# Second attention of a two-layer block: one of four score banks of four steps in eighteen is exponentiated on VectorE, and the products run four steps behind

## The reference, cut to what matters

```python
# four sequences of 1024 tokens, 128 channels, 16 heads of 8
xn = layernorm(x)
s = L0_attn(xn)                  # layer norm, qkv, softmax(q k / sqrt(8)) v, out projection, residual
g = silu(L0_ffn(xn))             # relu^2 MLP, five spiking steps, mean spike count
x = x + s * g
xn = layernorm(x)
# second layer
q, k, v = heads(xn @ W + bias)   # [4, 16, 1024, 8]
attn = q @ k.T / sqrt(8) - slope[h] * (1023 - key)
attn = where(causal, attn, -max)
p = softmax(attn)                # the exponentials that the change splits over two engines
s = (p @ v) @ Wo + bo
g = silu(L1_ffn(xn))             # three cycles of a coupling network
return x + s * g
```

## Time and profile before

| what | value |
|---|---|
| median of 3 runs | 917.85 us |
| profiled execution, its own time | 918.43 us |
| its span, first to last instruction | 916.5 us |
| mean granted TensorE clock | 0.973 |
| ACT busy, share of the span | 830.1 us, 91% |
| PE busy | 796.1 us, 87% |
| DVE busy | 406.5 us, 44% |
| POOL busy | 208.5 us, 23% |

### The profile page before, as it was taken

The page is one execution under the profiler, slowest core; times in us unless marked ns, Lnnn a source line. Parts: engine busy times, 40 slices in busy tenths (PEclk is TensorE's granted clock), DMA queues, the critical chain, the costliest instruction groups (busy, mean ns, idle before and its releaser), DMA issues. The chain is left out here.

```text
span 916.5 us, 23114 instructions
## 1 busy us (share of the span) xinstructions
PE 796.1 (87%) x9838; PEld 320.2 (35%) x9838; DVE 406.5 (44%) x878; ACT 830.1 (91%) x919; POOL 208.5 (23%) x261
## 2 busy tenths in 40 slices
PE   4849999899999999998999988856888888878977
PEld 2412434234343443433334433212333333333423
DVE  7821255443757446484545777880121121121122
ACT  7759999999999999999999956646999999999996
POOL 2201110130202212021211202002234334324333
PEclk9969999999999999999999999985999999999999
DMA  6882020200301202103000043010112022022000
GB/s 181 283 278 37 2 75 3 75 2 2 98 25 28 95 1 75 48 2 120 2 1 25 24 121 136 0 46 1 29 47 86 10 78 86 1 86 86 2 13 25
DMA packets 32048, 53.51 MB, mean 58 GB/s; under 512 B 5576, under 2 KB 16456, under 8 KB 31944
## 3 DMA queue, kind: packets, MB, share of 16 engines
q1 hardware_dynamic: 31944, 52.02, 18.0%
HBM read 31.29 MB, written 20.71 MB: 57 GB/s over the span
## 5 line engine op out<-in xcount | busy, mean ns | idle before, releaser
L973 ACT ACTIVATE a_probs<-a_sc 128x1024 f32<-128x1024 f32 x512 | 474.1, 1032 | 9.5 <-PE a_sc L1172 9.2
L1843 ACT ACTIVATE a_probs<-a_sc 128x1024 f32<-128x1024 f32 x288 | 270.0, 1041 | 23.8 <-PE a_sc L1995 17.2
L1187 PE MATMUL a_o<-a_probs,vt 128*18 128x256 f32 (+1 forms) x3072 | 271.6, 457 | 0.0
L2030 PE MATMUL a_o<-a_probs,vt 128*18 128x256 f32 (+3 forms) x1856 | 154.6, 442 | 0.9
L1172 PE MATMUL a_sc<-q_st,k_st 32*128 32x512 f32 x1024 | 131.0, 500 | 23.3 <-ACT a_probs L973 17.9
L1989 PE MATMUL a_sc<-q_st,k_st 32*128 32x512 f32 (+3 forms) x768 | 79.3, 428 | 56.8 <-ACT a_probs L1843 45.5
L1869 POOL TENSOR_SCALAR_AFFINE_SELECT a_probs<-a_probs 128x512 f32<-128x512 f32 x128 | 80.6, 648 | 194.7 <-ACT a_probs L1843 194.7
L1187 PEld LDWEIGHTS a_o<-a_probs,vt 128*18 128x18 f32 x3072 | 65.2, 97 | 143.2 <-issue 102.9
L1172 PEld LDWEIGHTS a_sc<-q_st,k_st 32*128 32x128 f32 x1024 | 50.4, 183 | 137.7 <-ACT a_probs L973 128.3
L1000 POOL TENSOR_TENSOR early<-early 128x512 f32<-128x512 f32 x32 | 38.3, 1198 | 179.2 <-DVE early L1110 179.2
L1902 DVE STREAM_TRANSPOSE a_turn<-a_o 128x512 f32<-128x512 f32 x15 | 10.8, 717 | 152.5 <-PE a_o L2030 152.5
(11 more groups left out here) (242 smaller groups left out, 754.9 us busy)
## 6 DMA issues: line engine op xcount, KB each, us to landing
q_st<-q_hl SPq DMA_DIRECT2D x48, 256.0 KB
k_st<-k_hl SPq DMA_DIRECT2D x48, 256.0 KB
q_hl<-parts SPq DMA_DIRECT2D x12, 512.0 KB, 4.3
k_hl<-parts SPq DMA_DIRECT2D x12, 512.0 KB, 4.7
q_hl<-early SPq DMA_DIRECT2D x4, 512.0 KB, 4.8
k_hl<-early SPq DMA_DIRECT2D x4, 512.0 KB, 5.2
out_dram<-x SPq DMA_DIRECT2D x7, 256.0 KB, 3.9
x<-in_L_attn_x_dram SPq DMA_DIRECT2D x3, 512.0 KB, 5.9
```

What stands on the lines that cost most here:

```text
L973: nc.scalar.activation(probs[t % RING][:, 2 * pair:2 * pair + 2, :], scores[unit % SLOTS][:, :, :], ACT.Exp).then_inc(expd, 1)
L1187: ins = nc.tensor.matmul(o_ps[32 * h:32 * h + 2 * W9, c0:c1], vt[b % 2][:, kt, gp, h, W9 * gs:W9 * gs + 2 * W9], probs[t % RING][:, h, c0: ...
L1843: nc.scalar.activation(probs[t % RING][:, 2 * pair:2 * pair + 2, :], scores[unit % SLOTS][:, :, :], ACT.Exp).then_inc(expd, 1)
L2030: ins = nc.tensor.matmul(o_ps[32 * h:32 * h + 2 * W9, q0:q0 + w], vt[b % 2][:, kt, gp, h, W9 * gs:W9 * gs + 2 * W9], probs[t % RING][:, h, ...
```

## The change

Four edits go together.

1. In the second attention the steps 5, 7, 14 and 16 of each group of 18 (`TAKES`) have their fourth head's bank exponentiated by DVE (`raise_head`): seven instructions that build the exponential from the bit pattern of a scaled score and a polynomial in its fraction. ACT's second ACTIVATE of such a step covers one head, 512 columns, in place of two. `score(t)` on PE also waits for the first of the seven instructions of step t-2, and `product(t)` for the last of its own step's.
2. LAG1 goes from 2 to 4 and the ring from 4 to 6. The two new buffers are the tiles `early`, and two scratch rows lie in `ext`.
3. In both attentions a multiply packs a lifted bank's used columns of both `gp` into one tile `gathered`, and only the second `gp` is transposed back. `on` has two tiles in place of four, the output weights are packed without zero rows (8 loads in place of 16, no memsets), and `mix` has half of the matmuls, in one piece: at pairs 4 and 15 of the second attention, 4 and 27 of the first.
4. At the end of the second attention four matmuls before the last two banks go away. POOL's early part of the last half (step 24) also waits for an earlier update.

```diff
+def gather(nc, ends, turned, recip, gathered, gp):
+    used = turned.rearrange("p (n r) -> p n r", r=32)[:, :, 0:2 * W9].rearrange("p n (s r) -> p n s r", r=W9)
+    ends.after(nc.vector.reciprocal(recip, used[:, :, :, D]))
+    blocks = turned.shape[1] // 32
+    ends.mark(nc.vector.tensor_tensor(gathered[:, :, gp, :, :], used[:, :, :, 0:D],
+                                      recip.rearrange("p n (s o) -> p n s o", o=1).broadcast_to([P, blocks, 2, D]), ALU.mult))
...
-            fill("mix", b - 1, 1, 3, 4)
+            fill("mix", b - 1, 1, 4)
...
-                    ends.after(nc.vector.reciprocal(recip[:, :, :], used[:, :, :, D]))
-                    ends.after(nc.vector.tensor_tensor(
-                        used, used, recip[:, :, :].rearrange("p n (s o) -> p n s o", o=1).broadcast_to([P, HALF // 32, 2, W9]), ALU.mult))
-                    nc.vector.transpose(on[e % ENDS][:, :], t[:, :]).then_inc(on_rdy, 1)
+                    gather(nc, ends, t[:, :], recip[:, :, :], s["gathered"][hf][:, :, :, :, :], gp)
+                    if gp == 1:
+                        ends.wait()
+                        nc.vector.transpose(on[hf][:, :], s["gathered"][hf][:, :, :, :, :].rearrange("p n g s d -> p (n g s d)")).then_inc(on_rdy, 1)
...
-                        pe.wait_ge(on_rdy, ENDS * b + 2 + hf + 1)
-                        for t in (2 * piece, 2 * piece + 1):
-                            for gp in range(2):
-                                ins = by_columns(nc, side_tiles[:, t, :], on[2 * gp + hf][:, t * P:(t + 1) * P],
-                                                 s["wo_x"][:, gp, :], start=gp == 0, stop=gp == 1)
+                        pe.wait_ge(on_rdy, 2 * b + hf + 1)
+                        for t in range(HT):
+                            ins = by_columns(nc, side_tiles[:, t, :], on[hf][:, t * P:(t + 1) * P], s["wo_x"][:, :])
...
                 for t in range(HT):
-                    for gp in range(2):
-                        ins = nc.tensor.matmul(pb[:, 1, t * C:(t + 1) * C], on[2 * gp + 1][:, t * P:(t + 1) * P],
-                                               s["wo_x"][:, gp, :], start=gp == 0, stop=gp == 1)
+                    ins = nc.tensor.matmul(pb[:, 1, t * C:(t + 1) * C], on[1][:, t * P:(t + 1) * P], s["wo_x"][:, :],
+                                           start=True, stop=True)
...
-LAG1 = 2
+LAG1 = 4
+RING1 = 6
 CORNER = 96
 STEEP = 1
+GROUP_STEPS = 18
+TAKES = (5, 7, 14, 16)
+TAKEN_HEAD = G - 1
+FRACTION, EXPONENT, ONE = 0x007FFFFF, 0x7F800000, 0x3F800000
+BITS_PER_E = float(np.float32(2.0 ** 23 / np.log(2.0)))
+BITS_OF_ONE = float(np.float32((127.0 - 6.2072499967381) * 2.0 ** 23))
+LEADING = 2.0 ** (BITS_OF_ONE / 2.0 ** 23 - 127.0)
+QUARTIC = [float(np.float32(c / LEADING)) for c in (-0.0021252070, 0.16661338, 0.31201603, 0.50996422)]
+POWER_OPS = 7
...
-            fill("mix", b - 1, 1, 3, 4)
+            fill("mix", b - 1, 1, 4)
...
-            fill("mix", b, 0, 14, 15)
...
-    LAST = S // 2 + 2
+    LAST = (S + LAG1) // 2 + 1
...
-        probs = [sb(f"probs{n}", [P, G, HALF]) for n in range(RING)]
+        late = [t[:, :, :, :].bitcast(F32).rearrange("p z n t -> p (z n) t") for t in s["early"]]
+        probs = [sb(f"probs{n}", [P, G, HALF]) for n in range(RING)] + late
+        bits, fraction = (s["ext"][0][:, HALF * n:HALF * n + HALF] for n in range(2))
...
+                    if t >= RING1:
+                        act.wait_ge(pv_done, t - RING1 + 1)
                     for pair in range(2):
                         unit = 2 * t + pair
                         act.wait_ge(scored, unit + 1)
-                        nc.scalar.activation(probs[t % RING][:, 2 * pair:2 * pair + 2, :],
-                                             scores[unit % SLOTS][:, :, :], ACT.Exp).then_inc(expd, 1)
+                        heads = 1 if by_vector(t) and pair == TAKEN_HEAD // 2 else 2
+                        nc.scalar.activation(probs[t % RING1][:, 2 * pair:2 * pair + heads, :],
+                                             scores[unit % SLOTS][:, 0:heads, :], ACT.Exp).then_inc(expd, 1)
...
-                    ends.after(nc.vector.reciprocal(recip[:, :, :], used[:, :, :, D]))
-                    ends.after(nc.vector.tensor_tensor(
-                        used, used, recip[:, :, :].rearrange("p n (s o) -> p n s o", o=1).broadcast_to([P, HALF // 32, 2, W9]), ALU.mult))
-                    nc.vector.transpose(on[e % ENDS][:, :], t[:, :]).then_inc(on_rdy, 1)
+                    gather(nc, ends, t[:, :], recip[:, :, :], s["gathered"][hf][:, :, :, :, :], gp)
+                    if gp == 1:
+                        ends.wait()
+                        nc.vector.transpose(on[hf][:, :], s["gathered"][hf][:, :, :, :, :].rearrange("p n g s d -> p (n g s d)")).then_inc(on_rdy, 1)
...
+                power = Chain(dve, powered)
+                def raise_head(t):
+                    unit = 2 * t + TAKEN_HEAD // 2
+                    out = probs[t % RING1][:, TAKEN_HEAD, :]
+                    if power.n:
+                        power.wait()
+                    dve.wait_ge(scored, unit + 1)
+                    power.after(nc.vector.tensor_scalar(bits.bitcast(U32), scores[unit % SLOTS][:, TAKEN_HEAD % 2, :],
+                                                        BITS_PER_E, BITS_OF_ONE, ALU.mult, ALU.add))
+                    power.mark(nc.vector.tensor_scalar(fraction.bitcast(U32), bits.bitcast(U32), FRACTION, ONE, ALU.bitwise_and, ALU.bitwise_or))
+                    power.after(nc.vector.tensor_scalar(bits.bitcast(U32), bits.bitcast(U32), EXPONENT, None, ALU.bitwise_and))
+                    if t >= RING1:
+                        dve.wait_ge(pv_done, t - RING1 + 1)
+                    power.after(nc.vector.scalar_tensor_tensor(out, fraction, QUARTIC[0], fraction, ALU.add, ALU.mult))
+                    power.after(nc.vector.scalar_tensor_tensor(out, out, QUARTIC[1], fraction, ALU.add, ALU.mult))
+                    power.after(nc.vector.scalar_tensor_tensor(out, out, QUARTIC[2], fraction, ALU.add, ALU.mult))
+                    power.mark(nc.vector.scalar_tensor_tensor(out, out, QUARTIC[3], bits, ALU.add, ALU.mult))
...
                 e = 0
@@ -1950,6 +1995,8 @@
                     ending = e < B * ENDS - 1 and 2 * pair - LAG1 > PER1 * (e // ENDS) + closing[e % ENDS]
                     if ending:
                         lift(e)
+                    if by_vector(2 * pair) and 2 * pair < S:
+                        raise_head(2 * pair)
                     for n, kind, at, hf, piece, pieces in pieces_at(pair):
                         if piece == pieces - 1:
                             evacuate(n, kind, at, hf)
@@ -1959,6 +2006,8 @@
                     for hf in range(2):
                         if b < B and r == GATE_AT[hf]:
                             gate(b, hf)
+                    if by_vector(2 * pair + 1) and 2 * pair < S:
+                        raise_head(2 * pair + 1)
...
-                    for unit in (2 * t, 2 * t + 1):
-                        if unit >= SLOTS:
-                            pe.wait_ge(expd, unit - SLOTS + 1)
+                    for unit in (2 * t - SLOTS, 2 * t + 1 - SLOTS):
+                        if unit >= 0:
+                            pe.wait_ge(expd, unit + 1)
+                            if by_vector(unit // 2) and unit % 2 == TAKEN_HEAD // 2:
+                                pe.wait_ge(powered, POWER_OPS * takes_before(unit // 2) + 1)
...
@@ -2021,6 +2072,8 @@
                             pe.wait_ge(masked, masked_count(t))
                         else:
                             pe.wait_ge(expd, 2 * t + 2)
+                        if by_vector(t):
+                            pe.wait_ge(powered, POWER_OPS * (takes_before(t) + 1))
                         if opens and t > 0:
...
-                        pe.wait_ge(on_rdy, ENDS * b + 2 + hf + 1)
-                        for t in (2 * piece, 2 * piece + 1):
-                            for gp in range(2):
-                                ins = by_columns(nc, side_tiles[:, t, :], on[2 * gp + hf][:, t * P:(t + 1) * P],
-                                                 s["wo_x1"][:, gp, :], start=gp == 0, stop=gp == 1)
+                        pe.wait_ge(on_rdy, 2 * b + hf + 1)
+                        for t in range(HT):
+                            ins = by_columns(nc, side_tiles[:, t, :], on[hf][:, t * P:(t + 1) * P], s["wo_x1"][:, :])
...
-                for t in range(HT):
-                    nc.tensor.matmul(tail_banks[t], on[1][:, t * P:(t + 1) * P], s["wo_x1"][:, 0, :], start=True, stop=False)
...
```

More of the change, by code:

```diff
@@ L846, in side_fills @@
         if b < B:
-            fill("mix", b, 0, 26, 27)
+            fill("mix", b, 0, 27)
         if 0 < b < B:
@@ L1742, in second_fills @@
             fill("z", b, 1, 7)
-            fill("mix", b, 0, 14, 15)
+            fill("mix", b, 0, 15)
     return fills
@@ L1804, in tail_tiles, with takes_before, by_vector @@
```

(12 more changed lines are left out.)

45 lines of the change are left out of this document (18 added, 27 removed).

## The result

| | before | after |
|---|---|---|
| median of 5 runs, same chip | 918.64 us (917.49 to 921.28) | 950.82 us (946.39 to 951.44) |
| profiled execution, span | 916.5 us | 944.1 us |
| mean granted TensorE clock | 0.973 | 0.956 |
| ACT busy, DVE busy | 830.1, 406.5 us | 818.9, 552.0 us |

The ratio is 1.034 with a 95% interval of 1.032 to 1.036: slower by 32 us, where 919.3 us were forecast, and outside the range of 907 to 929. The profiled execution of after is its shortest run, at 946.39 us. In the block, ACT's exponentials run from 622.5 us to about 930.5 us, where they ended at 907.9 before: 23 us more. Behind ACT's last one it takes another 13.6 us to the end of the span, where it took 8.6.

What follows compares the result with a forecast made beforehand. ACT was taken to set the pace: 918.43 - 13.1 (half units) - 4.3 (old stalls) + 17.0 (displaced work) + 3.0 (end) - 1.2 (middle block) = 919.8 us profiled, 919.3 us as median; 8-in-10 range 907 to 929 us.

Steps and rivals of the forecast that it cites:

- ACT's gain: Second attention: 32 units lose one bank, 0.41 us each, saving 13.1 us, with PE keeping up.
- the half unit is not worth 0.41 us: Rival on ACT's half units: saving 0.2 us less per unit leaves 6.7 us missing, partly hidden; 924 us, chance 0.04.
- Steps 14, 16, 32, 34: Second attention: second chain's first instruction, delayed by POOL's update, comes late for PE's scores; ACT loses 2.6 us.
- Chains held by POOL: Rival at the eight lift waits: masks hold chains 0.5 us each; 928 us, 936 with slow bit operations; chance 0.28.
- Steps 23, 25, 5 and 7: Second attention: lifts behind two chains delay PE's products; ACT loses 5.7 us (23, 25) and 8.7 us (5, 7).
- The end: End of second attention: later products and a last chain lengthened by POOL's update cost 3.0 us, bounds 1.9 and 3.7.
- the lag: At the end, products run two steps further behind: six after the last scores, not four, 2 x 0.87 us.
- POOL's part at step 24: Last half's early part: its added wait has only later masks behind it and costs nothing.
- at the start: Fewer PE products while the clock is 0.50: could save or cost 2 us, taken as nothing.
- DVE's chain: The seven DVE instructions of a take last 4.5 us, bounds 4.3 and 5.0.
- Old stalls: Second attention: ACT's losses at first query-half-1 diagonals, 1.24 us x 3 + 0.6 us, go: 4.3 us saved, bounds 0 and 4.3.
- the middle block: Between coupling layers, 16 matmul instructions become 8 at half clock: 1.2 us saved, bounds 1.25 and 0.

Runs made afterwards that it cites:

- E1: The changed kernel with no steps taken by DVE (TAKES empty), lag 4 and ring 6 kept: 915.88 us, ratio 0.996 to before.
- E7: The changed kernel with three polynomial steps left out of each DVE chain, four instructions in place of seven: 913.08 us, ratio 0.993 to before.
- E6: E3 with POOL's updates cut to 4 of 128 columns, leaving most of x without its addend: 920.89 us, ratio 1.002 to before.
- E3: The changed kernel with the lifts of parts 4 and 22 moved inside the second chain: 937.89 us, ratio 1.020 to before.
- E10: E7 with each score without triangle correction waiting for its two units apart: 909.62 us, ratio 0.989 to before.
- E11: The changed kernel, whole chains, with takes only at 6 and 16, half unit first, updates moved to steps 9 and 27: 909.86 us, ratio 0.989.
- E12: E11 with head 3 taken, so the half unit is second in its step: 914.34 us, ratio 0.995 to before.
- E4: The changed kernel with five filler matmuls on PE ahead of each wait for the lifts of parts 4 and 22: 948.02 us, ratio 1.032.
- E9: E7 with the half unit first in its step and takes at 6, 8, 14, 16: 908.6 us, ratio 0.987 to before.

## Why the prediction was wrong

The experiments make a stair from no takes to the change. Its steps stand beside the forecast's terms; the first term is what the forecast comes to without takes, 919.3 - 17.0 - 3.0 + 1.9 + 13.1 = 914.3, where 1.9 of the end's 3.0 us are the longer lag, which E1 keeps. The medians of before differ by up to 1.4 us between the groups used, so a step is good to about 1 us. Nor is each step one edit: from E7 to E6 the lifts move and the updates become narrow while the chains get their full length.

| step | from, to | measured | forecast | miss |
|---|---|---|---|---|
| rest of the change, no takes | E1 | 915.9 | 914.3 | +1.6 |
| 32 half units | E1, E7 | -2.8 | -13.1 | +10.3 |
| chains at full length, the end | E7, E6 | +7.8 | +1.1 | +6.7 |
| updates beside chains | E6, E3 | +17.0 | +2.6 | +14.4 |
| lifts behind two chains | E3, after | +12.9 | +14.4 | -1.5 |
| sum | | 950.8 | 919.3 | +31.5 |

*ACT's gain* is the first step that failed: "Saved: 0.41 x 32 = 13.1 us". The length was right (a 512-column unit takes 0.62 us), and ACT's busy time fell. I then compared PE's work per step with ACT's per step, 1.3 against 1.45 us, "PE keeps up". But a score is tied to single units, not to steps: it starts when the first unit ends, and the half unit behind it is shorter than the score's way to ACT. E7's rows, E10 and the pair E11/E12 bear this out. The rival "the half unit is not worth 0.41 us" named the effect, at 924 us and 0.04, but from a wrong cause, a longer instruction.

*Steps 14, 16, 32, 34* is the largest failure: 2.6 us stood for what came to 17. The mechanism was on the page, the sizes were not. I took the chain to be lengthened by 1.3 us. It was 1.9 us where an update met it, since both update instructions met one chain instruction each. The working doesn't name the evacuation between the two chains (0.6 us). And I took ACT's loss as 0.3 and 0.55 us, where it is 1.30 us and another 0.73 behind the fallen clock. Of the 17.0 us the traces put 13.7 in the block, for six meetings, and 3.6 behind ACT's last exponential, where the last update meets the chain of step 140. The Trainium skill (SBUF — State Buffer, Who interferes with whom) calls the port pair that the two engines share an exclusive lock. The trace agrees: 1.65 us beside an update instruction of 1.45 to 1.60, 0.69 alone. The rival "Chains held by POOL" had the right engine, but it put the price in the masks before the lifts and 0.5 us on each chain, and its 928 to 936 us stops short of the measured time.

*Steps 23, 25, 5 and 7* held: 14.4 us forecast, 12.9 measured, in the place that the forecast gave. The parts agree less well than the sum, which is luck in part. PE has seven such waits and not eight, four behind steps 23 and 25 of 1.5 (three) and 2.4 us for a forecast of 2.4, two behind 5 and 7 of 2.4 us for a forecast of 3.0, and one there of 1.23 us in the last batch (the profile puts it down to ACT, but it ends with the lift, at 875.5 us). ACT loses more at each than forecast: in the scene above 2.47 us at once and 1.30 us behind the clock. E4 puts the clock's own part at 3 us or less over the whole block. That part was not a term of the forecast; at the start it had a bound of 2 us either way, in mid-block none.

*The end* was sized at 3.0 us, 1.9 of it the lag; the tail behind ACT's last exponential grew by 5.0 us, 2.2 of it in E1 already, with the 2.51 us wait for the last chain. In the step of 7.8 us the tail has only 0.8. ACT has five waits in E6's trace that E7's lacks: 0.77, 0.76 and 0.54 us, once a batch, behind a product that waits up to 0.7 us for the last instruction of a second chain, and 1.31 and 0.64 us behind POOL's part at step 24. The forecast put that part at nothing because only masks come behind it in POOL's list; it had not asked which chain it runs beside. Some 3 of the 7.8 us stay open.

*DVE's chain* held: 0.69, 0.43, 0.42 and four of 0.69 us at 0.73 from start to start give 4.5 us undisturbed, the forecast's number.

*Old stalls, the middle block and the lag* held in sum: E1 gained 3.9 us on before by the medians, and the terms say 4.3 + 1.2 - 1.9 = 3.6. The 1.6 us in the table are little more than before's own 918.64 us here against 917.85. Term by term it is less clear. Of the 1.24 us at a batch's first query-half-1 diagonal, waits of 0.33 and 0.19 us remain, in E11 too. The middle block's 1.2 us can't be read from single traces, where ACT's first exponential of the block begins anywhere from 621.1 to 624.1 us (623.0 before). What E9's third and fourth takes cost stays open, for it has twice the half units of E11 and gains 1.3 us on it.

## What to carry to other kernels

Where an engine hands work back through a few slots, shortening one unit saves time only if the next unit is already there: walk the chain of slot, wait and reply for that very unit, and put the short one where a long one covers the reply. Work given to a second engine is priced by where it stands in that engine's list and whom it meets at SBUF, not by its busy share: the same update cost 2.4 us beside a chain and nothing that shows one step from it. Two takes in eighteen steps, with the half unit first and the updates out of the way, beat the change's four. Four whole chains placed as carefully, with the half unit first, were not run.

## What the runs showed of the hardware

- A DVE instruction with SBUF inputs took 1.65 us in place of 0.69 beside a POOL two-input instruction of 1.45 to 1.60 us, and did so once for each POOL instruction. A one-input DVE instruction on 512 columns took 0.86 us in place of 0.42 beside POOL's mask (L1983 at 729.69; two masks ran from 728.79 for 1.47 us), and 1.48 us beside a two-input POOL instruction of 1.43 us (L1983 at 903.55).
- PE's granted clock fell in mid-block behind idle times of 1.3 to 2.4 us (0.68 and 0.75 in 720 to 726 us, 0.53 in 738 to 741), and ACT then waited 0.7 to 1.3 us more. It did not fall each time (1.00 in 892 to 895 us behind 1.29 and 0.92 us). E1, which has no chains, has one such fall too: 0.64 in 767 to 770 us, behind a wait of 0.92 us, and ACT waited 1.50 us.
